# Row sums and squares in place of BN statistics, with a shifted edge: a fused gated-SSM and ternary FFN block

## The chip, the cores and the metric

The kernel runs on one core of a Trainium2 chip, in one launch. The metric is device time in microseconds, median of three executions. One more execution was recorded by the hardware profiler; every duration below comes from that one.

## The reference

The input is x, 8192 rows of 512 floats. Each layer is a norm, a block and a norm, with a residual around all three.

```python
x = x + _layernorm(attn(_layernorm(x)))
x = x + _layernorm(ffn(_layernorm(x)))
# attn: uv = x @ in_proj_w + in_proj_b; u, v = split(uv); v = silu(v)
#       v = 3-tap depthwise conv(v); h[t] = a*h[t-1] + ssm_b*v[t]; y = ssm_c*h + ssm_d*v
#       out = (u * silu(y)) @ out_proj_w + out_proj_b
#       h = out + residual; return layernorm(h) * ln_w + ln_b
# ffn:  h = gelu(x @ ternary(W1).T + b1);  return h @ ternary(W2).T + b2      (512 -> 2048 -> 512)
```

Between the two projections of one tile and its FFN stand three norms in a row: the norm inside `attn` (call it A, of out + residual), the norm around `attn` (B, whose input is A's output times ln_w plus ln_b), and the norm at the FFN's entrance (C, whose input is x1 = x + B). The second norm's input, in the words of the change, is the input of B.

## The kernel before

The 8192 rows are 16 tiles of 512 rows (`NT` = 16), each tile four blocks of 128 rows on the partitions (`NB` = 4, index j). All weights stay in SBUF. High precision comes from splitting a float into two float16 parts, `hi` (ScalarE) and `lo` (VectorE), so each projection is three matmuls where one would do.

The program is a software pipeline. In stage s, written `for s in LATER`, tile fa = s-2 is in its FFN, tile c = s-1 is in its SSM, out projection and norms A, B, C, tile n = s+1 is in its first norm and v projection, and tile e = s-3 gets the last touch of its FFN output and is stored. TensorE's order in a steady stage: nine f1 units of tile fa with five f2 units behind them (first half of the stage), the four u products of c, three more f2, the four o products of c, two v products of n, then f1 9 to 15 and the remaining f2, v 2 and 3, f2 12 to 15. `f1(t, j)` makes two hidden chunks for half a tile in bank `f1b`; ScalarE's `gelu` and `hi` and VectorE's `lo` make its float16 parts in `ring`; `f2(t, j)` multiplies them with W2 into the four banks `f2b`. f1 of unit i waits for gelu of i-2. u and o use two banks, `misc`, in turn: a product waits until the reader of the bank two products earlier is done (`gate` for u, `h_add` for o).

For tiles 2 to 12 (`seven(t)`), f2 is `f2_seven`: four plain matmuls over 512 columns for the `hi` part, and for the `lo` part seven half-size products in Strassen's manner, which need `combined` sums of W2 (made once, in `stage`) and four `presums` of two units of `h_lo`, made on VectorE (lines 970 to 977) just after `lo`. VectorE then takes the result apart with `drain`. Other tiles use plain products and `f_add`. Because tile fa's second half is drained in the next stage, `epilogue(e)` runs `f_add` or `drain`, `f_stats` and `aggr(4, ...)` early in it; GpSimd's `rstd_f` turns these into scales and ScalarE's `ffn_norm` waits for them.

The norms A, B, C of tile c on VectorE are `norms(c)`: `a1`, `a2` (A's output), `b_stats` and `aggr(2, ...)` (statistics of B's input), `x1`, `c_stats` and `aggr(3, ...)` (statistics of x1), `n3`. Between them GpSimd makes 1/sqrt of the variances (`rstd`, `rstd_b`), and afterwards the result is split (`t_hi`, `t_lo`) and transposed by DMA for the next f1.

The order on VectorE and ScalarE within a half stage is set by hand: each work item has a number (the `AT_` tables), and `run` sorts by it. The engines run their queues in order. An item that waits holds all behind it.

```python
def run(items):
    for _, work in sorted(items, key=lambda item: item[0]):
        work()
```

Stage 15 is special: tile 15 has no successor, so its SSM, u, o and `h_add` are done at the end of the same stage in which tile 14's norms run, and TensorE does all sixteen f2 units of tile 13 before them.

Of the kernel before, what the change touches and what calls it, by code (L numbers as in the profile page):

```python
# [63 lines left out]
AT_SILU_LAST, AT_GATE_LAST, AT_GATE_HI_LAST = 16.15, (15.0, 15.1), 16.5  # L64
AT_LO_LAST = (7.65, 8.95, 9.6, 10.6, 11.65, 12.2, 12.9)
# [36 lines left out]
def build(nc, x, w_in, w_out, w1t, w2t, params, rows, out):  # L102
# [42 lines left out]
    with ExitStack() as ctx:  # L145
# [389 lines left out]
        def _(pe):  # L535
# [50 lines left out]
            def o(c, j):  # L586

                out_ = take("o", c, j) if c > 0 else bank("o", 0, j)
# [58 lines left out]
            def f2_seven(t, j):  # L647
# [27 lines left out]
                product(f2b[0], right, s4, w2[:, p + PAIRS, right])
                product(f2b[1], left, a22, t4).then_inc(f2_mm, 1)

            def f2(t, j):
# [213 lines left out]
        def _(ve_):  # L892
# [37 lines left out]
            def f_add(e, j):  # L930
# [57 lines left out]
            def drain(t, h):  # L988
# [49 lines left out]
            def epilogue(e):  # L1038
# [1492 lines left out]
```

## Time and profile before

| | |
|---|---|
| median of 3 runs | 1414.5 us (1414.45 to 1415.38) |
| profiled execution | 1414.85 us, of which 1413.1 us span |
| TensorE busy | 1389.6 us, 98% |
| VectorE busy | 1208.9 us, 86% |
| ScalarE busy | 912.4 us, 65% |
| GpSimd busy | 371.8 us, 26% |
| TensorE clock granted | 0.999 of full speed |

A matmul's modelled end lies behind the start of the next, so short waits of TensorE do not show as idle time. They show as a start-to-start distance above the usual one. That usual distance is 0.216 us for 512 columns and 0.108 us for 256.

### The profile page before, as it was taken

How to read it: one execution, taken by the hardware profiler on the slowest of the kernel's cores; microseconds unless marked ns; L12 is line 12 of the kernel's file. 1: busy time of each engine (PE TensorE's matmuls, PEld its weight loads, DVE VectorE, ACT ScalarE, POOL GpSimd, SP SyncE). 2: the span in 40 equal slices, each digit the busy share in tenths (PEclk: the TensorE clock that was granted, in tenths of full speed). 3: DMA queues.
4: the chain of work that ended last, by engine and by line, in shares of the span. 5: the costliest groups of instructions: out<-in, count | busy, mean ns of one | idle time of the engine just before them, and what ended most of it. 6: DMA issues, size and time to landing. Idle time of an engine off the chain costs nothing.

```text
span 1413.1 us, 24900 instructions
## 1 busy us (share of the span) xinstructions
PE 1389.6 (98%) x8954; PEld 878.3 (62%) x8954; DVE 1208.9 (86%) x2360; ACT 912.4 (65%) x1504; POOL 371.8 (26%) x522
## 2 busy tenths in 40 slices
PE   7999999999999999999999999999999999999997
PEld 4444556657567675766757667675666757555664
DVE  7999988889889898888989889898898988898534
ACT  7999665756656565675656757566666656754543
POOL 5235242221412213132221412223132231313112
PEclk9999999999999999999999999999999999999999
DMA  8713530423304133232423305133141432202320
GB/s 237 256 45 90 137 54 19 109 42 91 60 12 109 31 90 61 45 75 31 107 44 91 51 11 120 31 90 60 26 96 31 97 53 61 31 1 63 58 30 31
DMA packets 164653, 98.12 MB, mean 69 GB/s; under 512 B 133681, under 2 KB 133681, under 8 KB 164401
## 3 DMA queue, kind: packets, MB, share of 16 engines
q1 hardware_dynamic: 155888, 80.79, 23.0%
q0 software_dynamic: 8640, 15.73, 8.2%
q8 instruction: 71, 1.16, 0.4%
q14 instruction: 54, 0.43, 0.1%
HBM read 31.49 MB, written 32.51 MB: 45 GB/s over the span
## 4 chain that ended last, share of the span: by engine, by line
PE 56%; DVE 19%; issue 11%; ACT 4%; POOL 3%; DVEq 0%; POOLq 0%; ACTq 0%
PE f1b L617 7%; PE f1b L618 7%; PE misc L580 5%; PE misc L582 5%; PE misc L581 5%; PE f2b L668 4%; DVE ring L926 4%; PE f2b L658 4%; PE misc L594 3%; PE f2b L641 3%; PE misc L596 3%; PE misc L595 3%; PE f2b L643 3%; DVE vl L1082 3%; DVE bn L908 2%
## 5 line engine op out<-in xcount | busy, mean ns | idle before, releaser
L618 PE MATMUL f1b<-x3T,w 128*128 128x256 f16 x1792 | 398.1, 273 | 0.0
L617 PE MATMUL f1b<-x3T,w 128*128 128x256 f16 x1792 | 398.1, 273 | 0.0
L1860 ACT ACTIVATE ring<-f1b,par 128x256 f32<-128x256 f32 x480 | 201.5, 471 | 208.3 <-PE f1b L618 208.0
L2297 POOL TENSOR_SCALAR ve<-mv 128x4 f32<-128x4 f32 (+2 forms) x89 | 46.9, 527 | 762.0 <-DVE mv L918 762.0
L926 DVE SCALAR_TENSOR_TENSOR ring<-ring,f_sc 128x512 f16<-128x512 f32 x256 | 188.0, 740 | 60.4 <-ACT ring L1874 60.4
L617 PEld LDWEIGHTS f1b<-x3T,w 128*128 128x128 fp8e5 x1792 | 175.4, 98 | 24.7 <-issue 0.4
L618 PEld LDWEIGHTS f1b<-x3T,w 128*128 128x128 fp8e5 x1792 | 175.3, 98 | 24.1
L1874 ACT ACTIVATE ring<-ring,f_sc 128x512 f16<-128x512 f32 x256 | 182.5, 720 | 0.0
L658 PE MATMUL f2b<-w,ring 128*128 128x512 fp8e5 x704 | 180.7, 379 | 0.0
L580 PE MATMUL misc<-x1T,win_hi 128*128 128x512 f16 x456 | 172.8, 379 | 1.8 <-DVE yb L1123 1.7
L582 PE MATMUL misc<-x1T,win_lo 128*128 128x512 f16 x456 | 172.8, 379 | 0.0
L581 PE MATMUL misc<-x1T,win_hi 128*128 128x512 f16 x456 | 172.8, 379 | 0.0
L1989 ACT ACTIVATE vb<-misc,par,inv_sig 128x512 f32<-128x512 f32 x54 | 41.9, 777 | 115.8 <-PE misc L582 115.7
L2354 POOL TENSOR_TENSOR hb<-hb,row 128x512 f32<-128x512 f32 x56 | 81.4, 1457 | 90.7 <-ACT hb L1921 90.7
L908 DVE BATCH_NORM_STATS2 bn<-hb 128x6 f32<-128x512 f32 x162 | 104.9, 680 | 0.2
L658 PEld LDWEIGHTS f2b<-w,ring 128*128 128x128 f16 x704 | 68.9, 98 | 50.2
L641 PE MATMUL f2b<-w,ring 128*128 128x512 fp8e5 x256 | 97.0, 379 | 0.9 <-DVE ring L926 0.8
L643 PE MATMUL f2b<-w,ring 128*128 128x512 fp8e5 x256 | 97.0, 379 | 0.0
L1082 DVE SCALAR_TENSOR_TENSOR vl<-vb,par,vl 128x512 f32<-128x512 f32 x128 | 92.4, 770 | 1.0 <-POOL vb L2403 0.8
L594 PE MATMUL misc<-wo_hi,g_hi 128*128 128x512 f16 x240 | 91.0, 379 | 0.4 <-DVE g_lo L1128 0.3
L595 PE MATMUL misc<-wo_lo,g_hi 128*128 128x512 f16 x240 | 91.0, 379 | 0.0
L596 PE MATMUL misc<-wo_hi,g_lo 128*128 128x512 f16 x240 | 91.0, 379 | 0.0
(263 smaller groups left out, 2695.1 us busy)
## 6 DMA issues: line engine op xcount, KB each, us to landing
out_dram<-xs SPq DMA_DIRECT2D x60, 256.0 KB, 2.9
xs<-x_dram SPq DMA_DIRECT2D x14, 1024.0 KB, 6.1
out_dram<-hb POOLq DMA_DIRECT2D x38, 256.0 KB, 5.2
out_dram<-stage POOLq DMA_DIRECT2D x22, 256.0 KB, 5.0
ring<-w1t_dram SPq DMA_DIRECT2D x3, 1024.0 KB, 12.3
stage<-w2t_dram SPq DMA_DIRECT2D x3, 1024.0 KB, 8.4
x1T<-tp SPq DMA_TRANSPOSE x68, 3.1
xs<-x_dram SPq DMA_DIRECT2D x4, 256.0 KB, 3.3
```

The lines of the kernel that those rows point to most:

```text
L580: pe.matmul(o[:, :], wh, x1T[:, s_, k, :], start=k == 0, stop=False)
L581: pe.matmul(o[:, :], wh, x1T[:, s_, KC + k, :], start=False, stop=False)
L582: mm = pe.matmul(o[:, :], wl, x1T[:, s_, k, :], start=False, stop=k == KC - 1)
L617: pe.matmul(o_, w, src[:, k, h * TH:(h + 1) * TH], start=k == 0, stop=False)
L618: mm = pe.matmul(o_, w, src[:, KC + k, h * TH:(h + 1) * TH], start=False, stop=k == KC - 1)
L641: pe.matmul(f2b[q][:, :], h_hi[:, i % H_SLOTS, qs], w2[:, chunk, :], start=chunk == 0, stop=False)
L643: mm = pe.matmul(f2b[q][:, :], h_lo[:, i % H_SLOTS, qs], w2[:, chunk, :], start=False, stop=chunk == FC - 1)
L658: pe.matmul(f2b[q][:, :], h_hi[:, r, n * TH + q * P:n * TH + (q + 1) * P], w2[:, chunk, :], start=p == 0 and n == 0, stop=False, skip_grou ...
L926: ve_.scalar_tensor_tensor(out=h_lo[:, i % H_SLOTS, :], in0=gg[:, i % G_SLOTS, :], scalar=f_sc[:, 0:1], in1=h_hi[:, i % H_SLOTS, :], op0=A ...
L1082: ve_.scalar_tensor_tensor(out=dst, in0=src, scalar=w, in1=dst, op0=ALU.mult, op1=ALU.add).then_inc(done, 1)
L1860: ins = act.activation(gg[:, i % G_SLOTS, ts], f1b[i % 2][:, ts], ACT.Gelu, bias=par[:, B1 + chunk:B1 + chunk + 1], scale=1.0 / ACT_SCALE)
L1874: act.activation(h_hi[:, i % H_SLOTS, :], gg[:, i % G_SLOTS, :], ACT.Copy, scale=f_sc[:, 0:1]).then_inc(hh_ok, 1)
```

## The change

Seven edits, named by letters.

(a) In `f2_seven` the wait for `sums_ok` moves back by three products: the three that use only `h_lo` come first, behind a wait for `hl_ok`. (b) `middle(t)` adds tile 1 to the tiles whose first output half is kept in `stage` (`hb_first`) and finished in the same stage. Tile 1's `f_add` and `f_stats` of blocks 0 and 1 move from stage 4 into stage 3, and those of blocks 2 and 3 stand before the scans. (c) For tiles 2 to 13 (`summed`) `a2` and `x1` write a row sum beside their result; `b_stats`, `c_stats` and their `aggr` are gone; ScalarE runs a Square with accumulation over each block, eight a tile; GpSimd makes the mean from the sum and the variance from the squares, with one more instruction for each norm. (d) In stage 15 three `lo` and two `t_lo` items and a gate change their places. (e) GpSimd's four `add_bias` of tile 15 go from behind tile 14's norms to two earlier places, behind waits for `a2` and `x1`. (f) The last out projection does three quarters of blocks 0 and 1, then their last quarters. (g) `h_add` of blocks 0 and 1 of tile 15 comes earlier among tile 13's `f_add`.

```diff
-AT_LO_LAST = (7.65, 8.95, 9.6, 10.6, 11.65, 12.2, 12.9)
+AT_LO_LAST = (7.65, 8.95, 9.6, 10.6, 11.6, 11.65, 12.2)
...
+AT_NORM_SUMS = ((7.7, 7.95, 8.2, 8.45), (8.7, 8.8, 8.9, 9.0), (11.7, 11.95, 12.2, 12.45), (14.7, 14.95, 15.2, 15.45))
+AT_B_SQUARE, AT_C_SQUARE = (9.05, 10.15, 11.15, 12.15), (13.15, 13.16, 14.15, 14.16)
...
+    def middle(t):
+
+        return 0 < t < NT - 3
+
+    def summed(c):
+
+        return 1 < c < NT - 2
...
-                pe.wait_ge(sums_ok, 4 * rank(i) + 4)
+                pe.wait_ge(hl_ok, i + 1)
...
                 product(f2b[0], left, a12, w2[:, p + PAIRS, left])
+                product(f2b[1], left, a22, t4)
+                pe.wait_ge(sums_ok, 4 * rank(i) + 4)
                 product(f2b[3], right, s1, t1, p == 0)
...
-                product(f2b[0], right, s4, w2[:, p + PAIRS, right])
-                product(f2b[1], left, a22, t4).then_inc(f2_mm, 1)
+                product(f2b[0], right, s4, w2[:, p + PAIRS, right]).then_inc(f2_mm, 1)
...
-                    for j in range(NB):
-                        o(NT - 1, j)
+                    o(NT - 1, 0, range(0, KC - 1))
+                    o(NT - 1, 1, range(0, KC - 1))
+                    o(NT - 1, 0, range(KC - 1, KC))
+                    o(NT - 1, 1, range(KC - 1, KC))
+                    o(NT - 1, 2)
+                    o(NT - 1, 3)
...
-                at = AT_F_STATS_NEXT if seven(e + 1) else AT_F_STATS
+                if middle(e):
+                    return (spread(AT_F_ADD, .2, [lambda j=j: f_add(e, j) for j in range(2, NB)])
+                            + spread(AT_F_STATS_SEVEN, .001, [lambda j=j: f_stats(e, j) for j in range(2, NB)])
+                            + spread(AT_F_STATS_SEVEN + .004, .001, [lambda j=j: aggr(4, e, j) for j in range(2, NB)]))
...
-                                             in1=lnb_row, op0=ALU.mult, op1=ALU.add).then_inc(a2_ok, 1)
+                                             in1=lnb_row, op0=ALU.mult, op1=ALU.add,
+                                             accum_out=sum_b[:, j:j + 1] if summed(c) else None).then_inc(a2_ok, 1)
...
+                if summed(c):
+                    at = AT_NORM_SUMS
+                    return [(at[k][j], lambda f=f, j=j: f(j)) for k, f in enumerate((a1, a2, x1, n3)) for j in range(NB)]
...
+                    gate_lo(NT - 1, 2)
                     gate(NT - 1, 3)
-                    gate_lo(NT - 1, 2)
+                    t_lo("t3", NT - 2, 1)
                     gate_lo(NT - 1, 3)
                     t_lo("t3", NT - 2, 2)
                     t_lo("t3", NT - 2, 3)
                     f_add(NT - 3, 0)
+                    h_add(NT - 1, 0)
+                    h_add(NT - 1, 1)
                     f_add(NT - 3, 1)
-                    h_add(NT - 1, 0)
...
+                src = hb_of(c)[:, j, :] if of_b else xs[:, c % X_SLOTS, j, :]
+                act.activation(spare[:, j % 2, :], src, ACT.Square, bias=sums[:, j:j + 1], scale=-float(D),
+                               accum_out=squares[:, j:j + 1], saturate=False).then_inc(done, 1)
...
+            def mean_of(sums, dst, made, c):
+
+                pool.wait_ge(made, NB * (c + 1))
+                link(pool.tensor_scalar(dst[:, :], sums[:, :], 1.0 / D, None, ALU.mult))
+
+            def rstd_sums(ln, squares, ready, c, dst, last):
+
+                pool.wait_ge(ready, NB * (c - 1))
+                link(pool.tensor_scalar(ve[:, ln, :], squares[:, :], 1.0 / D ** 3, EPS, ALU.mult, ALU.add))
+                ins = pool.tensor_tensor(dst, ve[:, ln, :], mhalf[:, :], ALU.pow)
...
+                if s == NT - 1:
+                    pool.wait_ge(a2_ok, NB * (c + 1))
+                    add_bias(NT - 1, 0)
+                    add_bias(NT - 1, 1)
                 if c is not None:
                     rstd_b(c)
+                if s == NT - 1:
+                    pool.wait_ge(x1_ok, NB * (c + 1))
+                    add_bias(NT - 1, 2)
+                    add_bias(NT - 1, 3)
```

**Place 1, edit (b).** VectorE's queue in the first half of stage 4, before, from the end of the second pair of taps (line 1082) over the first two scans (1091), `lo` and presums, to tile 1's FFN statistics (908, 918):

```order
L1082 SCALAR_TENSOR_TENSOR vl<-vb,par,vl 128x512 [waits tap0] x2
L1091 SCALAR_TENSOR_TENSOR vl<-a_par,carry,vl 128x512 [waits carry_ok,dv_ok,tap2]
L926 SCALAR_TENSOR_TENSOR ring<-ring,f_sc 128x512 [waits hh_ok]
L1091 SCALAR_TENSOR_TENSOR vl<-a_par,carry,vl 128x512 [waits carry_ok,dv_ok,tap2]
L926 SCALAR_TENSOR_TENSOR ring<-ring,f_sc 128x512 [waits hh_ok]
L974 TENSOR_TENSOR stage<-ring 128x2x128 [waits f2_mm,hl_ok]
L975 TENSOR_TENSOR stage<-ring 128x2x128
L977 TENSOR_TENSOR stage<-ring,stage 128x2x128 [waits sums_ok]
L970 TENSOR_TENSOR stage<-ring,stage 128x2x128 [waits sums_ok]
L908 BN_STATS bn<-hb 128x6 [waits mv_ok4,f_ok] x4
L918 BN_AGGR mv<-bn 128x2 [waits rs_ok4,bn_ok4] x4
```

The same place in the changed program, from the same taps on:

```order
L1113 SCALAR_TENSOR_TENSOR vl<-vb,par,vl 128x512 [waits tap0] x2
L935 BN_STATS bn<-hb 128x6 [waits mv_ok4,f_ok] x2
L945 BN_AGGR mv<-bn 128x2 [waits rs_ok4,bn_ok4] x2
L1122 SCALAR_TENSOR_TENSOR vl<-a_par,carry,vl 128x512 [waits carry_ok,dv_ok,tap2]
L953 SCALAR_TENSOR_TENSOR ring<-ring,f_sc 128x512 [waits hh_ok]
L1122 SCALAR_TENSOR_TENSOR vl<-a_par,carry,vl 128x512 [waits carry_ok,dv_ok,tap2]
L953 SCALAR_TENSOR_TENSOR ring<-ring,f_sc 128x512 [waits hh_ok]
L1003 TENSOR_TENSOR stage<-ring 128x2x128 [waits f2_mm,hl_ok]
L1004 TENSOR_TENSOR stage<-ring 128x2x128
L1006 TENSOR_TENSOR stage<-ring,stage 128x2x128 [waits sums_ok]
L999 TENSOR_TENSOR stage<-ring,stage 128x2x128 [waits sums_ok]
```

Four statistics behind the first two scans have become two in front of them; the other two now stand in stage 3.

**Place 2, edit (c).** ScalarE's queue in the second half of a steady stage of the changed program; `ring<-f1b` is a half of a gelu, `ring<-ring` is `hi`, `vl<-vb` is the centre tap of the next tile, and `xn,sq_b` and `xn,sq_c` are the squares:

```order
L1913 ACTIVATE ring<-ring,f_sc 128x512 [waits f2_mm,gelu_ok]
L1976 ACTIVATE xn,sq_b<-hb,sum_b 128x512 [waits bsq_ok,x1_lo,a2_ok]
L1899 ACTIVATE ring<-f1b,par 128x256 [waits hl_ok,f1_mm]
L1899 ACTIVATE ring<-f1b,par 128x256
L1913 ACTIVATE ring<-ring,f_sc 128x512 [waits f2_mm,gelu_ok]
L1976 ACTIVATE xn,sq_b<-hb,sum_b 128x512 [waits bsq_ok,x1_lo,a2_ok]
L1899 ACTIVATE ring<-f1b,par 128x256 [waits hl_ok,f1_mm]
L1899 ACTIVATE ring<-f1b,par 128x256
L1913 ACTIVATE ring<-ring,f_sc 128x512 [waits f2_mm,gelu_ok]
L1976 ACTIVATE xn,sq_c<-xs,sum_c 128x512 [waits bsq_ok,x1_lo,x1_ok] x2
L1938 ACTIVATE vl<-vb,par 128x512 [waits carry_ok,y_ok,v_ok] x2
L1899 ACTIVATE ring<-f1b,par 128x256 [waits hl_ok,f1_mm]
```

Without the rows that write `xn` this is the order before. The two first squares of x1 stand in front of two centre taps and a gelu, and they wait for VectorE's `x1` (the semaphore `x1_ok`).

**Place 3, edits (d) and (g).** VectorE's queue at the end of stage 15, before, from `lo` (926) of f2 unit 13 on; 1182 is `x1`, 1191 `n3`, 1123 `gate`, all as above:

```order
L926 SCALAR_TENSOR_TENSOR ring<-ring,f_sc 128x512 [waits hh_ok]
L1182 SCALAR_TENSOR_TENSOR xs<-hb,rsc,xs 128x512 [waits rs_ok2]
L1182 SCALAR_TENSOR_TENSOR xs<-hb,rsc,xs 128x512 x2
L926 SCALAR_TENSOR_TENSOR ring<-ring,f_sc 128x512 [waits hh_ok]
L1182 SCALAR_TENSOR_TENSOR xs<-hb,rsc,xs 128x512
L908 BN_STATS bn<-xs 128x6 [waits mv_ok3,x1_ok]
L926 SCALAR_TENSOR_TENSOR ring<-ring,f_sc 128x512 [waits hh_ok]
L908 BN_STATS bn<-xs 128x6 [waits mv_ok3,x1_ok] x3
L918 BN_AGGR mv<-bn 128x2 [waits rs_ok3,bn_ok3] x4
L1191 TENSOR_SCALAR hb<-xs,mv,rsc 128x512 [waits rs_ok3]
```

And in the changed program, from the same unit on:

```order
L953 SCALAR_TENSOR_TENSOR ring<-ring,f_sc 128x512 [waits hh_ok] x2
L1214 SCALAR_TENSOR_TENSOR xs<-hb,rsc,xs 128x512 [waits rs_ok2]
L1214 SCALAR_TENSOR_TENSOR xs<-hb,rsc,xs 128x512 x2
L953 SCALAR_TENSOR_TENSOR ring<-ring,f_sc 128x512 [waits hh_ok]
L1214 SCALAR_TENSOR_TENSOR xs<-hb,rsc,xs 128x512
L935 BN_STATS bn<-xs 128x6 [waits mv_ok3,x1_ok] x4
L945 BN_AGGR mv<-bn 128x2 [waits rs_ok3,bn_ok3] x4
L1225 TENSOR_SCALAR hb<-xs,mv,rsc 128x512 [waits rs_ok3]
L1154 SCALAR_TENSOR_TENSOR yb<-misc,bu_sig,yb 128x512 [waits u_mm,sy_ok]
L1225 TENSOR_SCALAR hb<-xs,mv,rsc 128x512
```

The `lo` of unit 14 has moved in front of the wait for `rs_ok2`, unit 15's has moved in front of the last `x1`, and a gate stands between the first two `n3`.

## Rows read from the trace of the kernel before

**Rows 1.** Busy time by window, core 0: a steady stage, stage 15, the rest.
```profile
682.08:767.42 85.34, 85.25 (x579) 56.24 (x576) 75.68 (x155) 54.88 (x92) 21.29 (x30) 1.00 0.30 62
...
1194.10:1293.24 99.14, 97.89 (x578) 55.91 (x576) 88.26 (x136) 57.11 (x96) 25.18 (x28) 1.00 0.22 47
1293.24:1413.10 119.86, 111.31 (x769) 75.05 (x767) 60.30 (x112) 56.20 (x111) 22.86 (x39) 0.99 0.20 36
```

**Rows 2.** Who waited for whom: total us, times, longest; weight loads of line 668.
```profile
PEld f2b L668 <- DVE stage L970: 8.6, 21, 0.6
```

**Rows 3.** Timeline, TensorE: start us, us, what [idle before <-releaser], stage 4.
```profile
282.57 0.38 PE L582 MATMUL misc<-x1T,win_lo 128*128 128x512 f16 x1
284.70 0.39 PE L580 MATMUL misc<-x1T,win_hi 128*128 128x512 f16 x1 [1.75 <-DVE yb L1123]
```

**Rows 4.** Timeline, VectorE and ScalarE, first half of stage 4.
```profile
268.70 2.47 DVE L908 BATCH_NORM_STATS2 bn<-hb 128x6 f32<-128x512 f32 x4
...
275.70 1.52 ACT L1885 ACTIVATE hb<-hb,nm,rs 128x512 f32<-128x512 f32 x2 [4.82 <-POOL nm L2329]
...
283.23 1.67 ACT L1926 ACTIVATE yb<-yb 128x512 f32<-128x512 f32 x3
...
283.89 1.41 DVE L1123 SCALAR_TENSOR_TENSOR yb<-misc,bu_sig,yb 128x512 f32<-128x512 f32 x2
```

**Rows 5.** Timeline, TensorE and VectorE, one f2 unit early in a steady stage.
```profile
782.90 1.03 PE L658 MATMUL f2b<-w,ring 128*128 128x512 fp8e5 x4
...
783.68 0.29 DVE L970 TENSOR_TENSOR stage<-ring,stage 128x256 f16<-128x256 f16 x1
...
784.03 0.39 PE L668 MATMUL f2b<-w,ring 128*128 128x256 fp8e5 x2
```

**Rows 6.** Timeline, TensorE, end of stage 15.
```profile
1266.73 0.38 PE L643 MATMUL f2b<-w,ring 128*128 128x512 fp8e5 x1
1267.95 0.39 PE L641 MATMUL f2b<-w,ring 128*128 128x512 fp8e5 x1 [0.84 <-DVE ring L926]
...
1283.93 0.39 PE L594 MATMUL misc<-wo_hi,g_hi 128*128 128x512 f16 x1 [0.31 <-DVE g_lo L1128]
```

**Rows 7.** Timeline, VectorE and GpSimd, end of stage 15.
```profile
1262.91 0.72 DVE L926 SCALAR_TENSOR_TENSOR ring<-ring,f_sc 128x512 f16<-128x512 f32 x1
1265.16 2.08 DVE L1182 SCALAR_TENSOR_TENSOR xs<-hb,rsc,xs 128x512 f32<-128x512 f32 x3 [1.52 <-POOL c L2321]
...
1273.36 2.90 DVE L1191 TENSOR_SCALAR hb<-xs,mv,rsc 128x512 f32<-128x512 f32 x2 [1.48 <-POOL rsc L2298]
...
1273.29 5.33 POOL L2354 TENSOR_TENSOR xs<-xs,row 128x512 f32<-128x512 f32 x4
```

**Rows 8.** Groups by line and shape: busy us, mean ns of one, idle before.
```profile
L908 DVE BATCH_NORM_STATS2 bn<-hb 128x6 f32<-128x512 f32 x162 | 104.9, 680 | 0.2
...
L1147 DVE SCALAR_TENSOR_TENSOR hb<-misc,o_inv,hb 128x512 f32<-128x512 f32 x56 | 41.7, 744 | 3.3 <-PE misc L596 2.2
...
L1182 DVE SCALAR_TENSOR_TENSOR xs<-hb,rsc,xs 128x512 f32<-128x512 f32 x60 | 41.3, 746 | 8.1 <-POOL c L2321 8.0
...
L918 DVE BATCH_NORM_AGGREGATE mv<-bn 128x2 f32<-128x6 f32 x320 | 40.9, 165 | 0.2
...
L1899 ACT ACTIVATE vl<-vb,par 128x512 f32<-128x512 f32 x64 | 48.9, 808 | 0.1
...
L1999 ACT ACTIVATION_READ_ACCUMULATOR w<-ring 128x1 f32 x4 | 0.8, 192 | 0.0
```

**Rows 9.** Timeline, ScalarE and VectorE, second half of a steady stage.
```profile
740.69 0.84 ACT L1860 ACTIVATE ring<-f1b,par 128x256 f32<-128x256 f32 x2 [0.56 <-PE f1b L618]
...
744.18 0.84 ACT L1860 ACTIVATE ring<-f1b,par 128x256 f32<-128x256 f32 x2 [0.30 <-PE f1b L618]
...
750.14 2.74 DVE L1182 SCALAR_TENSOR_TENSOR xs<-hb,rsc,xs 128x512 f32<-128x512 f32 x4 [0.48 <-POOL c L2321]
...
759.39 1.46 DVE L1191 TENSOR_SCALAR hb<-xs,mv,rsc 128x512 f32<-128x512 f32 x3 [1.47 <-POOL rsc L2298]
```

More of the change, by code:

```diff
@@ L372, in fo_pair @@
         def fo_pair(t, h):
-            return hb_first if seven(t) and h == 0 else hb[:, 2 * h:2 * h + 2, :]
+            return hb_first if middle(t) and h == 0 else hb[:, 2 * h:2 * h + 2, :]
         def fo(t, j):
@@ L584, in in_proj, with o @@
                     mm.then_inc(done, 1)
-            def o(c, j):
-                out_ = take("o", c, j) if c > 0 else bank("o", 0, j)
+            def o(c, j, ks=range(KC)):
+                out_ = take("o", c, j) if c > 0 and ks[0] == 0 else bank("o", c, j)
                 js = slice(j * P, (j + 1) * P)
@@ L591, in o @@
                     pe.wait_ge(wo_l, KC)
-                for k in range(KC):
+                for k in ks:
                     pe.wait_ge(glo_ok, KC * c + k + 1)
@@ L1761, in _ @@
                     gate_lo(c, 3)
-                parts = drain(fa, 0) if seven(fa) else []
+                parts = drain(fa, 0) if seven(fa) else [lambda j=j: f_add(fa, j) for j in range(2)] if middle(fa) else []
                 if n is not None:
@@ L1814, in _ @@
                 if c is not None:
-                    items += [(at, lambda j=j: t_lo("t3", c, j)) for j, at in enumerate(AT_T3_LO) if s < NT - 1 or j < 2]
+                    items += [(at, lambda j=j: t_lo("t3", c, j)) for j, at in enumerate(AT_T3_LO) if s < NT - 1 or j < 1]
                 if s == NT - 1:
@@ L1922, in residual, with square @@
                                scale=rs1[:, c % 4, j:j + 1]).then_inc(res_ok, 1)
+            def square(c, j, of_b):
+                sums, squares, made, done = (sum_b, sq_b, a2_ok, bsq_ok) if of_b else (sum_c, sq_c, x1_ok, csq_ok)
+                i = NB * (c - 2) + j
+                act.wait_ge(made, NB * c + j + 1)
+                act.wait_ge(x1_lo, NB * (c + 3))
+                if j >= 2:
+                    act.wait_ge(done, i - 1)
+                elif of_b and c > 2:
+                    act.wait_ge(csq_ok, i - j)
+                elif not of_b:
+                    act.wait_ge(bsq_ok, i - j + NB)
+                src = hb_of(c)[:, j, :] if of_b else xs[:, c % X_SLOTS, j, :]
+                act.activation(spare[:, j % 2, :], src, ACT.Square, bias=sums[:, j:j + 1], scale=-float(D),
+                               accum_out=squares[:, j:j + 1], saturate=False).then_inc(done, 1)
             def silu_y(c, b):
@@ L2235, in _ @@
                 if e is not None:
-                    items += [(at, lambda j=j: ffn_norm(e, j)) for j, at in enumerate(AT_F_NORM_SEVEN if seven(e) or seven(e + 1) else AT_F_NORM)]
+                    items += [(at, lambda j=j: ffn_norm(e, j)) for j, at in enumerate(AT_F_NORM_SEVEN if middle(e) else AT_F_NORM)]
                 if c is not None and s < NT:
@@ L2270, in _ @@
                     items += [(at, lambda b=b: centre_tap(s, b)) for b, at in enumerate(AT_CENTRE)]
+                if summed(c or 0):
+                    items += [(at, lambda j=j: square(c, j, True)) for j, at in enumerate(AT_B_SQUARE)]
+                    items += [(at, lambda j=j: square(c, j, False)) for j, at in enumerate(AT_C_SQUARE)]
                 if c is not None:
@@ L2488, in _ @@
                     rstd(1, c, rsc[:, 0, :], True)
+                if s == NT - 1:
+                    pool.wait_ge(a2_ok, NB * (c + 1))
+                    add_bias(NT - 1, 0)
+                    add_bias(NT - 1, 1)
                 if c is not None:
                     rstd_b(c)
+                if s == NT - 1:
+                    pool.wait_ge(x1_ok, NB * (c + 1))
+                    add_bias(NT - 1, 2)
+                    add_bias(NT - 1, 3)
+                if summed(c or 0):
+                    mean_of(sum_c, mean_c, x1_ok, c)
+                    rstd_sums(3, sq_c, csq_ok, c, rsc[:, 2, :], True)
+                elif c is not None:
                     rstd(3, c, rsc[:, 2, :], True)
-                if s == NT - 1:
-                    for j in range(NB):
-                        add_bias(NT - 1, j)
                 if n is not None:
```

56 lines of the change are left out of this document (39 added, 17 removed).

## The prediction

> **What bounds the kernel now.** I read the busy time by window first. In a steady stage TensorE is busy for 85.25 of 85.34 us, VectorE for 75.68, ScalarE for 54.88 [rows 1]. TensorE's stream sets the length of a stage; another engine matters only where TensorE waits for it. So the gain to be had is the sum of those waits, and I read the timeline of TensorE for start-to-start distances above 0.216 us (512 columns) or 0.108 us (256). Behind the start-up there are three kinds.
>
> First, one small stop in each of ten stages, at the weight loads of the f2 unit that opens a stage. The waits name it: line 668 behind VectorE's presum, 21 times, longest 0.6 us [rows 2]; most of the 8.6 us lie in weight loads that run ahead and cost nothing. On the timeline, the four matmuls from 782.90 are through at 782.90 + 4 x 0.216 = 783.76; the next starts at 784.03, since the last presum ended at 783.97 [rows 5]. That is 0.27 us, and I read 0.26 to 0.27 in the ten stages from 356.9 to 1124.9: 2.64 us together.
>
> Second, stage 4: 282.57 to 284.70 is 2.13 us where 0.22 is usual, so 1.91 lost, waiting for a gate [rows 3].
>
> Third, the end of stage 15: 1266.73 to 1267.95 is 1.22, so 1.01 lost behind a `lo`; before 1283.93 0.47 is lost behind a split gate [rows 6]; the same view has three smaller ones, 0.18, 0.18 and 0.23, nothing after that. Sum 2.07.
>
> All together 2.64 + 1.91 + 2.07 = 6.6 us. No edit takes work from TensorE, so 6.6 is about the most that the change can bring.
>
> **Edit (a), the order in `f2_seven`.** Same seven products. Those in front of the wait grow by three times 0.108 = 0.32 us. In the unit of [rows 5] the presums are then wanted at 783.76 + 0.32 = 784.08, and were ready at 783.97. The 0.27 us is covered with 0.11 to spare, if VectorE doesn't deliver later. Its queue ahead of that presum is not lengthened: the norms of the previous tile, shortened by (c), stand before it. Ten times 0.264: **-2.64 us**.
>
> **Edit (b), stage 4.** The chain is in [rows 4]: four statistics from 268.70 to 271.17, their four aggregations, GpSimd's scale; ScalarE's `ffn_norm` idles 4.82 us for it at 275.70 and holds `silu_y` behind it until 283.23; `gate` at 283.89 to 285.30; TensorE stands for 1.91. The change takes two `f_add` (0.74 each), two statistics (0.62) and two aggregations (0.08 start to start) from VectorE here, some 2.9 us, and puts the other statistics in front of the scans. Two scans and two `lo` (about 4 x 0.72 = 2.9 us) no longer stand before them. The scale is there some 4.5 to 5 us earlier, about the 4.82 that ScalarE idled, and the gate is wanted 1.9 us earlier. In the steady stages, whose statistics already stand in this place, the same wait is absent. Stage 3 pays for it: two `f_add`, two statistics and two aggregations more on VectorE, 2.9 us, while (c) takes more than that from the same half. **-1.91 us**.
>
> **Edit (c), sums and squares in twelve tiles.** VectorE loses eight statistics and eight aggregations. Four statistics in a row take 2.47 [rows 4], so 0.62 each; with 0.08 for an aggregation, 8 x 0.70 = 5.6 us a tile. It gains the output of eight sums. No row shows VectorE writing one. Bounds: 0, and 0.19 us, which ScalarE's own read of its accumulator takes as an instruction [rows 8]; I take 0.1, so 0.8 a tile, and VectorE is 4.8 us a stage lighter. ScalarE gains eight squares of 128x512. The nearest row is the activation of that size, 808 ns from start to modelled end [rows 8], about 0.63 to 0.71 from start to start, and about 0.1 for the accumulator: 8 x 0.75 = 6 us on 54.88 of 85.34 [rows 1]. GpSimd gets two small operations more, about 0.5 each. All three stay below TensorE, so there is no direct gain and no direct loss, but the order matters. Squares of B's input stand between a `hi` and the next gelu. In [rows 9] gelu waits for TensorE, by 0.56 at 740.69 and 0.30 at 744.18, so half of a square disappears in such idle time and the rest shifts gelu by about 0.1 to 0.4; `f1` of the unit after next wants it 0.7 us after it was done. Squares of x1 wait for VectorE's `x1` with two centre taps and a gelu behind them. `x1` at 750.14 waits 0.48 and `n3` at 759.39 waits 1.47 for GpSimd [rows 9]. Now the chain is: last `a2`, last square (about 747.1), GpSimd 2.2 us, `x1` at about 749.3; and `n3` at about 757.5. Both are earlier. The gelu behind the two squares comes 2.2 us later, but the f1 unit that takes its bank stands behind two v products and three f2 units and is not due before about 764. **0 us**; the cover is this slack of 0.7 us at the tightest gelu, and each 0.1 us beyond it costs 1.2 us in twelve tiles.
>
> The price of the sum bears on a rule. In [rows 8] the operation with two SBUF sources (line 1182, `x1`) takes 746 ns, that with a PSUM source (line 1147) 744: no sign that two SBUF sources are slower. The Trainium skill, "Vector Engine (DVE) Microarchitecture Reference", section 7, says that this kind of operation with two non-bf16 SBUF sources runs at half throughput, since both read ports are taken and none is left for the accumulator; the rows contradict it without a sum, and no row has one. What such a halving would do is rival B.
>
> **Edits (d), (e), (f), (g), stage 15.** The `lo` that TensorE waited for started at 1267.2 or so, behind three `x1` that had idled 1.52 for GpSimd; at 1262.91 VectorE had just done the previous `lo` and had that idle time to give [rows 7]. Now the next one stands in it: -1.01, and the one after it stands before the last `x1`: -0.18. The first two `n3` took 2.90 beside GpSimd's `add_bias` [rows 7], 1.45 each, against 1.46 / 3 = 0.49 in a steady stage [rows 9]; with `add_bias` elsewhere VectorE gains up to 1.9 us, `t_lo` and gates are earlier by as much, and the three smaller stops (0.18, 0.47, 0.23) close. That is -2.07. Against it: the split of the last o product puts the start of o(15, 2) behind o(15, 0) by only three matmuls of 0.216, 0.65 us, and it needs the bank that `h_add` of block 0 reads (0.74 us with its start). VectorE can begin only at the end of o(15, 0), so TensorE stands for about 0.35 including the semaphore. I put **-2.07 + 0.35 = -1.72**. What follows TensorE's end, some 8.5 us, stays.
>
> **Sum.** -2.64 - 1.91 + 0 - 1.72 = -6.27. The profiled execution took 1414.85 us (span 1413.1), so 1408.6; it lies 0.35 above the median of the runs, 1414.5, from which the sum gives 1408.2. I say 1408.3.
>
> **The rivals.** **B, the sum costs VectorE a second pass.** If `a2` goes from 0.66 to 1.2 us start to start, four of them delay the squares and, more, the `lo` and presums of f2 unit 8, ready at 744.0 before and wanted at 745.2 with edit (a); four times 0.54 with what queues behind gives about 745.4, 0.25 us a tile. Twelve tiles: +3.0, so 1411.3. The rows of [rows 8] speak against it, as far as they go. The Trainium skill's rule of the same section would give this case. Chance 0.12.
>
> **C, an edit frees only part of its stop.** In stage 4 `silu_y` could stay late because ScalarE's own `d_conv` and `hi` stand before it, in stage 15 the gates; the 1.52 and 1.48 us waits for GpSimd [rows 7] remain, and `add_bias` now stands before the `rstd(3)` that `n3` waits for. Half of 1.91 and half of 1.72 lost: +1.8, so 1410.1. Chance 0.12.
>
> **D, slower: the squares of x1 hold ScalarE.** They wait for `x1_ok` with gelu behind. Place: the second half of each of twelve tiles. The slack is the distance from the end of that gelu, about 758.8, to the next use at 764 or later, and 0.7 us at the earlier gelus. It decides once the chain a2, squares, GpSimd, x1 slips by more than that. If squares cost 1.5 us instead of 0.75, gelus of f1 10 to 13 are late by 0.8 to 1 us against 0.7, and four such waits a tile of 0.2 give 12 x 0.8 = 9.6: 1408.3 + 9.6 = 1418. For it: four squares of B's input stand in the densest part of ScalarE's queue. Against it: nothing in the rows puts an activation of this size above 0.81. Chance 0.05.
>
> **E, no gain in the steady stages.** Small shifts of gelu or `lo` open new stops of about 0.3 us as large as those closed: 2.6 + 1 back, so 1412. Chance 0.05.
>
> **How the numbers follow.** A measurement of this kernel tells 0.2%, 2.8 us, from no change: faster is below 1411.7, slower above 1417.3. My forecast, 0.66, with its own range 1407.4 to 1409.4: below, all 6.6 us plus 0.3 for gaps in the start-up; above, the 0.35 doubled and one of the small stops left. B 0.12 at 1411.3, C 0.12 at 1410.1, E 0.05 at 1412, D 0.05 at 1418. The range is 1407.3 to 1411.5: it takes in the forecast, C and most of B. Faster: the forecast, C, and most of B, 0.88; same: E and a part of B, 0.07; slower: D, 0.05.
>
> **What the profile of the changed kernel would show.** (a) Steady f2 units without a distance above 0.22 at the first products, or one of a few hundredths. (b) At 282 to 285 no gap, `ffn_norm`'s idle time below 1 us. (c) `a2` and `x1` still near 745 ns with a small extra each, VectorE's busy time in a steady stage about 71, ScalarE's about 61 to 62, a stage 85.07 us long instead of 85.34. (d) No idle time before line 641 at the place of 1267.95; (e) the first `n3` near 0.5 us each; (f) a new stop of 0.3 to 0.4 before o(15, 2). The prediction is wrong if a steady stage is longer than 85.15 us, above all if `a2` takes 1.2 us, if `gelu` waits for the squares of x1 into f1's time, or if stage 15 has a new wait behind `h_add` of more than half a microsecond.

## The result, and the profile after

The changed kernel takes 1409.13 us (median of 6 runs, 1407.68 to 1411.74), the kernel before on the same chip 1414.38 us (6 runs, 1413.37 to 1415.38). The ratio is 0.9963, 95% interval 0.9951 to 0.9975: 5.25 us, or 0.37%, faster. The profiled execution took 1408.3 us with a span of 1406.5, against 1414.85 and 1413.1. The six runs of the changed kernel spread over 4 us, so a median says less about the edits than the trace does.

In the trace I use one sum throughout: how far TensorE's start-to-start distances from 100 us on exceed 0.216 us (512 columns) or 0.108 us (256). It leaves out the start-up, which differs by 1 to 2 us between executions. Before, this sum is 12.56 us, of which 7.06 in stops above 0.1 us; after, it is 6.17, of which 0.72 in two stops. So the sum has fallen by 6.4 us, nearly all of it in stops, and two stops are left: 0.36 us at 109 us, which both kernels have, and 0.36 us in stage 15. One trace stands behind each kernel. Places that no edit touches move by up to 0.1 us between traces (the stop at 253.4 us, 0.12 here, is 0.11 with edit (a) alone and 0.22 with (d) to (g) alone), and one trace has a stop of 0.38 us that no other has. I therefore read a small difference at its place and not off the sum.

A steady stage is 85.10 us instead of 85.34 [rows 1] (busy time by window, columns as there: TensorE, its weight loads, VectorE, ScalarE, GpSimd, granted clock):

```profile
679.00:764.10 85.10, 85.10 (x579) 56.36 (x578) 70.82 (x146) 59.85 (x108) 21.93 (x32) 1.00 0.30 63
```

VectorE is 4.86 us a stage lighter, ScalarE 4.97 us heavier. In their stages tile 8's `x1` starts 1.5 us earlier than before and its `n3` 2.7 us earlier. TensorE's f2 unit that answers to [rows 5], with VectorE's last presum (timeline; start, duration):

```profile
779.47 1.03 PE L680 MATMUL f2b<-w,ring 128*128 128x512 fp8e5 x4
780.33 0.38 PE L690 MATMUL f2b<-w,ring 128*128 128x256 fp8e5 x2
780.55 0.27 PE L690 MATMUL f2b<-stage,ring 128*128 128x256 fp8e5 x1
780.66 0.49 PE L690 MATMUL f2b<-stage 128*128 128x256 fp8e5 x3
...
780.15 0.29 DVE L999 TENSOR_TENSOR stage<-ring,stage 128x256 f16<-128x256 f16 x1
```

The four plain matmuls (line 680) are through at 779.47 + 0.86 = 780.33, and the first product starts there. The sums end at 780.44, after that start and 0.22 us before 780.66, where the first product that reads them begins.

ScalarE in stage 4, against [rows 4], where `ffn_norm` idled 4.82 us:

```profile
270.61 1.51 ACT L1924 ACTIVATE stage<-stage,nm,rs 128x512 f32<-128x512 f32 x2
272.64 0.84 ACT L1899 ACTIVATE ring<-f1b,par 128x256 f32<-128x256 f32 x2 [0.53 <-PE f1b L640]
...
273.98 1.51 ACT L1924 ACTIVATE hb<-hb,nm,rs 128x512 f32<-128x512 f32 x2
...
279.39 2.19 ACT L1981 ACTIVATE yb<-yb 128x512 f32<-128x512 f32 x4
```

Both pairs of `ffn_norm` run without a wait, and the four `silu_y` run from 279.39 on, where before they began at 283.23. TensorE's stop of 1.91 us is gone.

VectorE at the end of stage 15, against [rows 7], and TensorE's one new stop:

```profile
1258.12 1.39 DVE L953 SCALAR_TENSOR_TENSOR ring<-ring,f_sc 128x512 f16<-128x512 f32 x2
1260.72 2.08 DVE L1214 SCALAR_TENSOR_TENSOR xs<-hb,rsc,xs 128x512 f32<-128x512 f32 x3 [1.21 <-POOL c L2399]
...
1268.25 0.55 DVE L1225 TENSOR_SCALAR hb<-xs,mv,rsc 128x512 f32<-128x512 f32 x1 [1.47 <-POOL rsc L2356]
1268.71 0.74 DVE L1154 SCALAR_TENSOR_TENSOR yb<-misc,bu_sig,yb 128x512 f32<-128x512 f32 x1
...
1280.93 0.38 PE L617 MATMUL misc<-wo_hi,g_lo 128*128 128x512 f16 x1
1281.51 0.39 PE L615 MATMUL misc<-wo_hi,g_hi 128*128 128x512 f16 x1 [0.20 <-DVE xs L1178]
```

Two `lo` now stand in front of the wait for GpSimd, `n3` takes 0.55 us, and the third o product waits for `h_add`: 1281.51 - 1280.93 - 0.22 = 0.36 us.

The operations of edit (c) (groups by line and shape: busy us, mean ns of one):

```profile
L1214 DVE SCALAR_TENSOR_TENSOR xs<-hb,rsc,xs 128x512 f32<-128x512 f32 x60 | 41.7, 747 | 12.7 <-POOL c L2396 11.4 <-POOL c L2399 1.2
L1203 DVE SCALAR_TENSOR_TENSOR hb<-hb,rsc,row 128x512 f32<-128x512 f32 x60 | 41.6, 746 | 0.0
...
L1976 ACT ACTIVATE xn<-hb,sum_b 128x512 f16<-128x512 f32 x48 | 35.0, 730 | 0.3 <-DVE hb L1203 0.3
...
L1976 ACT ACTIVATION_READ_ACCUMULATOR xn<-hb,sum_b 128x1 f32 x48 | 10.0, 208 | 0.0
...
L1203 DVE DVE_READ_ACCUMULATOR hb<-hb,rsc,row 128x1 f32 x48 | 4.0, 84 | 0.0
```

And how they follow each other (timeline, VectorE, one `a2` and the next, then ScalarE):

```profile
735.60 0.09 DVE L1203 DVE_READ_ACCUMULATOR hb<-hb,rsc,row 128x1 f32 x1
735.60 0.75 DVE L1203 SCALAR_TENSOR_TENSOR hb<-hb,rsc,row 128x512 f32<-128x512 f32 x1
736.27 0.09 DVE L1203 DVE_READ_ACCUMULATOR hb<-hb,rsc,row 128x1 f32 x1
...
736.58 0.72 ACT L1976 ACTIVATE xn<-hb,sum_b 128x512 f16<-128x512 f32 x1
737.19 0.20 ACT L1976 ACTIVATION_READ_ACCUMULATOR xn<-hb,sum_b 128x1 f32 x1
737.28 0.83 ACT L1899 ACTIVATE ring<-f1b,par 128x256 f32<-128x256 f32 x2
```

An `a2` with its row sum takes 0.67 us from start to start, and its accumulator is read in the same moment in which the next one starts. A square holds ScalarE for 737.28 - 736.58 = 0.70 us.

### The profile page after: what moved, and what is told of

The parts are those of the page before. It is cut to its first block, busy times and chain, and to the rows that moved or that the text cites. A ratio compares the mean times of both kernels' runs of the same rounds, so it can differ in the third digit from the quotient of the medians.

```text
span 1406.5 us, 24951 instructions
## 1 busy us (share of the span) xinstructions
PE 1386.9 (99%) x8954; PEld 879.9 (63%) x8954; DVE 1148.1 (82%) x2264; ACT 971.7 (69%) x1696; POOL 379.1 (27%) x546
## 4 chain that ended last, share of the span: by engine, by line
PE 92%; DVE 1%; issue 0%; ACT 0%; POOLq 0%; POOL 0%; DVEq 0%; ACTq 0%
PE f1b L639 15%; PE f1b L640 15%; PE f2b L680 11%; PE f2b L690 10%; PE misc L603 7%; PE misc L602 7%; PE misc L601 7%; PE f2b L665 4%; PE f2b L663 4%; PE misc L615 4%; PE misc L617 4%; PE misc L616 4%; PE f2b L722 1%; PE f2b L723 1%; PE f1b L645 0%; PE f1b L646 0%
## 5 line engine op out<-in xcount | busy, mean ns | idle before, releaser
L2355 POOL TENSOR_SCALAR ve<-mv 128x4 f32<-128x4 f32 (+2 forms) x65 | 35.5, 547 | 529.1 <-DVE mv L945 529.0
L1989 ACT ACTIVATE g_hi<-yb,g_sc 128x512 f16<-128x512 f32 x64 | 45.5, 716 | 71.2 <-DVE yb L1154 71.2
```

## The experiments

All times are medians beside the kernel before on the same chip (1414.36, 1414.40 and 1414.39 us in the three batches); "excess" is TensorE's sum from 100 us on. Edits are given against the kernel named.

| kernel | median us | ratio to before (95%) | excess us |
|---|---|---|---|
| before | 1414.4 | | 12.56 |
| changed | 1409.1 | 0.9963 (0.9951 to 0.9975) | 6.17 |
| (a) alone | 1411.6 | 0.9981 (0.9972 to 0.9990) | 9.83 |
| (b) alone | 1412.9 | 0.9988 (0.9979 to 0.9996) | 11.21 |
| (d) to (g) alone | 1412.6 | 0.9986 (0.9977 to 0.9995) | 10.76 |
| (c) alone | 1413.7 | 0.9994 (0.9985 to 1.0003) | 11.56 |
| changed without (c) | 1408.8 | 0.9965 (0.9953 to 0.9977) | 6.60 |
| changed without (f) | 1408.4 | 0.9964 (0.9951 to 0.9976) | 6.50 |
| changed without (e) | 1408.9 | 0.9963 (0.9949 to 0.9977) | 7.39 |
| changed, o in another bank | 1407.7 | 0.9959 (0.9946 to 0.9971) | 5.81 |
| changed, all squares twice | 1470.4 | 1.0395 (1.0381 to 1.0410) | 69.2 |
| changed, squares of B's input twice | 1421.9 | 1.0054 (1.0039 to 1.0069) | 20.06 |
| changed, squares of x1 twice | 1424.0 | 1.0068 (1.0053 to 1.0083) | 22.12 |

**(a) alone.** Against before:

```diff
-                pe.wait_ge(sums_ok, 4 * rank(i) + 4)
+                pe.wait_ge(hl_ok, i + 1)
...
+                product(f2b[1], left, a22, t4)
+                pe.wait_ge(sums_ok, 4 * rank(i) + 4)
                 product(f2b[3], right, s1, t1, p == 0)
```

> The kernel before with edit (a) alone. Theory: the three products cover the 0.27 us stop by themselves (margin 0.11 us), so the ten stops are gone and the span is 2.6 us shorter, time about 1411.8, VectorE as before. Rival: (a) needs the lighter VectorE of (c); the sums are then late by 0.1 to 0.2 us and a stop of that size is left ten times, gain only 1 to 2 us.

1411.58 us, excess 2.74 us down. None of the ten stops is left, the others stand as they were. The same unit as in [rows 5] (timeline, TensorE):

```profile
781.44 1.03 PE L658 MATMUL f2b<-w,ring 128*128 128x512 fp8e5 x4
782.31 0.38 PE L668 MATMUL f2b<-w,ring 128*128 128x256 fp8e5 x2
```

781.44 + 0.86 is 782.30: no gap. The edit needs no lighter VectorE.

**(b) alone.** Against before, with the branch for `middle` in `epilogue` and `f_add` as in the full diff:

```diff
+    def middle(t):
+
+        return 0 < t < NT - 3
...
-            return hb_first if seven(t) and h == 0 else hb[:, 2 * h:2 * h + 2, :]
+            return hb_first if middle(t) and h == 0 else hb[:, 2 * h:2 * h + 2, :]
```

> The kernel before with edit (b) alone. Theory: the 1.91 us stop in stage 4 is gone and stage 3 gets none, gain 1.9 us, time about 1412.5. Rival: the two more f_add, statistics and aggregations in stage 3 lie on a VectorE that (c) has not relieved, and a new stop of 0.3 to 1.9 us appears in stage 3 or 4; gain under 1.6 us.

1412.85 us. The 1.91 us stop is gone, but the excess falls by 1.35 only. At 253.3 us the stop before the first f1 of stage 4 has grown from 0.12 to 0.64, and one of 0.17 has come at 270.3, before products that read sums. The rival was right: VectorE in stage 3 isn't free without (c).

**(d) to (g) alone.** Against before, with the calls in stage 15 as in the full diff:

```diff
-AT_LO_LAST = (7.65, 8.95, 9.6, 10.6, 11.65, 12.2, 12.9)
+AT_LO_LAST = (7.65, 8.95, 9.6, 10.6, 11.6, 11.65, 12.2)
```

> The kernel before with edits (d), (e), (f), (g), all in stage 15. Theory: the five stops of 2.07 us go and one of 0.36 before the third o product comes, gain 1.7 us, time about 1412.7, independent of the rest. Rival: stage 15 is entered later or earlier relative to VectorE than with the others, and a stop of 0.2 to 0.5 us is left behind a lo.

1412.56 us, excess 1.80 down: five stops of 2.07 us gone, one of 0.36 new, so 1.71 in stops. The remaining 0.09 us is within what differs between traces.

**(c) alone.** The changed kernel with (a), (d) to (g) taken back as above, and (b) by:

```diff
     def middle(t):
-        return 0 < t < NT - 3
+        return 1 < t < NT - 3
```

> The kernel before with edit (c) alone. Theory: VectorE is about 4.5 us lighter and ScalarE 5 to 6 us heavier in each of twelve tiles, and TensorE's stops stay, those of line 668 at most 0.1 us smaller each because VectorE is a little earlier: span 0 to 1 us shorter, time 1413.5 to 1414.4, the 1.91 and the 2.07 us unchanged. Rival: the lighter VectorE already has the sums ready, the ten stops vanish with it and (a) would have been needless: 2.6 us shorter.

1413.68 us: not told from before by time. By the trace the excess is 1.00 down. Each of the ten stops is 0.17 to 0.18 instead of 0.26 to 0.27 (0.85 us in all), the one of 0.12 at 253.4 is gone, and those of stages 4 and 15 are unchanged.

**The changed kernel without (c).**

```diff
     def summed(c):
-        return 1 < c < NT - 2
+        return False
...
     def turn(ln, t):
-        return t - (max(0, t - 2) if t < NT - 2 else NT - 4) if ln in (2, 3) else t
+        return t
```

(`turn` gives the counts that the waits for statistics use.)

> The changed kernel with BN statistics in all tiles, so without edit (c). Theory: (c) bears nothing of the gain, TensorE has the same single stop of 0.36 us, span within 0.3 us of the changed kernel, time about 1408.4. Rival: (c) gave part of it, as the margin of the sums (0.11 us by the count) is used up, stops of 0.1 to 0.2 us in ten stages, 1 to 2 us slower than the changed kernel.

1408.8 us, the same by time. By the trace one stop has come back, 0.53 us at 253.4, before the first f1 of stage 4:

```profile
253.45 0.38 PE L665 MATMUL f2b<-w,ring 128*128 128x512 fp8e5 x1
254.20 0.27 PE L639 MATMUL f1b<-x3T,w 128*128 128x256 f16 x1 [0.37 <-issue]
```

It reads tile 2's transposed n3. The first `n3` of that tile starts at 246.75 here, at 244.32 with (c), and at 246.34 in the kernel before (timeline, VectorE, in this order; then TensorE before):

```profile
246.75 1.46 DVE L1225 TENSOR_SCALAR hb<-xs,mv,rsc 128x512 f32<-128x512 f32 x3 [1.24 <-POOL rsc L2356]
...
244.32 1.46 DVE L1225 TENSOR_SCALAR hb<-xs,mean_c,rsc 128x512 f32<-128x512 f32 x3 [1.21 <-POOL rsc L2385]
...
246.34 1.46 DVE L1191 TENSOR_SCALAR hb<-xs,mv,rsc 128x512 f32<-128x512 f32 x3 [1.24 <-POOL rsc L2298]
...
253.41 0.38 PE L643 MATMUL f2b<-w,ring 128*128 128x512 fp8e5 x1
253.75 0.27 PE L617 MATMUL f1b<-x3T,w 128*128 128x256 f16 x1
```

With (c) `n3` comes 2.4 us earlier, against a stop of 0.5. Against the kernel before, `n3` comes 0.41 us later here and the stop is 0.41 us longer. I read the wait from what f1 waits for in the code and from these times; the trace names no releaser.

**The changed kernel without (f).**

```diff
-                    o(NT - 1, 0, range(0, KC - 1))
-                    o(NT - 1, 1, range(0, KC - 1))
-                    o(NT - 1, 0, range(KC - 1, KC))
-                    o(NT - 1, 1, range(KC - 1, KC))
-                    o(NT - 1, 2)
-                    o(NT - 1, 3)
+                    for j in range(NB):
+                        o(NT - 1, j)
```

> The changed kernel with the four last o products whole and in order, so without edit (f). Theory: the 0.36 us stop before the third o product goes, and one behind the last split gate comes back, since g_lo of block 3 ends about 0.45 us before its place with the split and TensorE wants it three matmuls times three, 1.9 us, earlier: net 1 to 1.5 us slower. Rival: (e) and the moved gates already have that part ready, and the split only costs its 0.36 us: 0.3 us faster.

Neither: the 0.36 us stop is gone and one of 0.68 stands inside the first o product (at 1277.5), so the split is worth 0.32 us. I had the direction, not the size. The median, 1408.36, can't tell 0.3 us.

**The changed kernel without (e).**

```diff
-                if s == NT - 1:
-                    pool.wait_ge(a2_ok, NB * (c + 1))
-                    add_bias(NT - 1, 0)
-                    add_bias(NT - 1, 1)
...
-                if s == NT - 1:
-                    pool.wait_ge(x1_ok, NB * (c + 1))
-                    add_bias(NT - 1, 2)
-                    add_bias(NT - 1, 3)
...
+                if s == NT - 1:
+                    for j in range(NB):
+                        add_bias(NT - 1, j)
```

> The changed kernel with GpSimd's four add_bias of tile 15 behind tile 14's norms again, so without edit (e). Theory: the first two n3 take 1.45 us each again, gates and splits of stage 15 come up to 1.9 us later, and stops of 0.2 to 0.9 us in all come back before u and o products: 0.2 to 0.9 us slower. Rival: the order of gates and lo alone closes them, and the span is the same within 0.1 us apart from the start-up.

The first `n3` takes 1.49 us again, and stops of 0.11, 0.23 and 0.82 us stand in stage 15 in place of the 0.36: 0.8 us more, as expected. (The excess holds a further 0.38 us at 1068 us that no other trace has; what it waits for is open.)

```profile
1268.39 1.49 DVE L1225 TENSOR_SCALAR hb<-xs,mv,rsc 128x512 f32<-128x512 f32 x1 [1.47 <-POOL rsc L2356]
```

**Another bank for one o product.** The first of the last four goes to bank `f1b` 0, idle there; the third then waits for a gate only.

```diff
+                if (kind, t, i) == ("o", NT - 1, 0):
+                    pe.wait_ge(gelu_ok, FC * (NT - 2) - 1)
+                    return bank(kind, t, i)
+                if (kind, t, i) == ("o", NT - 1, 2):
+                    pe.wait_ge(reader["u"], 4 * (NT - 1) + i + 1)
+                    return bank(kind, t, i)
...
+                if (t, j) == (NT - 2, 0):
+                    pe.wait_ge(h_ok, NB * (NT - 1) + 1)
```

> The changed kernel with the first of the last four o products in the bank f1b 0, which is idle there, so that the third waits for a gate that was done long before and not for h_add. Theory: the last stop of 0.36 us goes, span 0.36 us shorter, time about 1408.0. Rival: the stop moves to the fourth o product or to the first f1 behind, and the time stays.

From 112 us to the end no stop above 0.1 us is left; the excess is 5.81, the least of all. 1407.66 us, 0.9959 of before: the best version run, though its interval overlaps that of the changed kernel.

**All squares twice.** This doubles the work of the step that the prediction's slower case rests on; the second result overwrites the first.

```diff
-                act.activation(spare[:, j % 2, :], src, ACT.Square, ...).then_inc(done, 1)
+                for k in range(SQUARES):
+                    ins = act.activation(spare[:, j % 2, :], src, ACT.Square, ...)
+                    if k < SQUARES - 1:
+                        extra[0] += 1
+                        ins.then_inc(again, 1)
+                        act.wait_ge(again, extra[0])
+                ins.then_inc(done, 1)
```

> The changed kernel with each Square done twice (the first result is overwritten), sixteen a tile. ScalarE gets about 6 us more in each of twelve stages. Theory by the margins of f1 behind gelu in the changed kernel (0.68, 2.02 and 3.36 us at the units 12, 13 and 14): the gelus are late by 0.75, 1.5 and 2.2 us, so 0.1 us is lost at unit 12 and what the longer chain to x1 and n3 brings is hidden: 1 to 2 us slower in all. Rival, the slower case of the prediction: the squares of x1 hold gelu and hi of units 13 and 14 past their use, 0.8 us or more a tile, 10 us slower or more.

1470.4 us, 61 us slower than the changed kernel. Both expectations fall. The gelus give way where the margins said, at f1 unit 12, by one stop of 0.22 us a tile (2.4 us in all). The large loss is elsewhere, eleven times in this form (timeline, TensorE; then VectorE one tile later, 90 us on):

```profile
611.09 1.04 PE L682 MATMUL f2b<-w,ring 128*128 128x512 fp8e5 x4 [0.21 <-ACT ring L1915]
...
612.21 0.27 PE L692 MATMUL f2b<-stage,ring 128*128 128x256 fp8e5 x1
615.36 0.82 PE L692 MATMUL f2b<-stage 128*128 128x256 fp8e5 x3 [2.88 <-DVE stage L1001]
...
616.19 1.91 PE L682 MATMUL f2b<-w,ring 128*128 128x512 fp8e5 x4
...
696.92 0.29 DVE L1001 TENSOR_TENSOR stage<-ring,stage 128x256 f16<-128x256 f16 x1
699.99 1.46 DVE L1227 TENSOR_SCALAR hb<-xs,mean_c,rsc 128x512 f32<-128x512 f32 x3 [2.77 <-POOL rsc L2395]
701.36 0.75 DVE L955 SCALAR_TENSOR_TENSOR ring<-ring,f_sc 128x512 f16<-128x512 f32 x1
...
705.19 0.29 DVE L1001 TENSOR_TENSOR stage<-ring,stage 128x256 f16<-128x256 f16 x1
```

VectorE stands 2.77 us at `n3`, which waits for GpSimd's scale, which waits for ScalarE's last square. Behind `n3` in its queue are the `lo` and the presums of f2 units 14 and 15, and TensorE stands for them 3.04 us. The chain from `a2` to `n3` has become 6.4 us longer: 3.15 from `a2` to `x1`, 3.26 from `x1` to `n3`.

Then the clock. After that stop four matmuls of 512 columns take from 616.19 to 617.89, 0.43 us each and not 0.22: TensorE runs at 1.2 GHz (busy time by window; the last three columns are granted clock, DMA share and GB/s):

```profile
612.30:615.30 3.00, 0.18 (x2) 0.00 (x0) 2.93 (x8) 2.97 (x5) 0.00 (x0) 0.93 0.49 94
615.40:618.90 3.50, 3.50 (x16) 1.96 (x17) 3.01 (x5) 2.37 (x3) 0.32 (x2) 0.58 0.80 154
619.00:622.00 3.00, 3.00 (x30) 2.69 (x28) 2.93 (x7) 0.84 (x2) 0.00 (x0) 1.00 1.18 292
```

The mean granted clock of the window behind the stop is 0.58; it is 0.50 from 614.9, shortly before the stop ends, to 618.3. The sum over the excess: 11 x 3.04 = 33.5 for the stop, 4.1 for one of 0.37 just ahead of it, 14.5 for half-clock stretches in eight of the eleven tiles, 2.2 for a stop of 0.73 in the three others, 2.4 at unit 12, 4.7 in stage 3, the rest small.

**Either half of the squares twice.** In the kernel above, `SQUARES` for B's input and for x1 apart; (1, 2) in the second run:

```diff
-SQUARES = 2
+SQUARES = (2, 1)
```

> The changed kernel with only the four squares of B's input done twice. In the run with all eight doubled, x1 and n3 together came 6.4 us later than before behind a2, TensorE stood 3.4 us a tile for presums whose lo stands behind n3, and ran at half clock for some 3 us after it. Theory: one chain with a slack of about 3.0 us decides; this half lengthens it by 3.15, so 0.1 to 0.4 us a tile, no clock drop, 2 to 5 us slower than the changed kernel, about 1412. Rival, linear: each half gives half of the 61 us, about 1440; and if the gelus between these squares were what counts, nearly all of it, 1460.

> The changed kernel with only the four squares of x1 done twice. Theory of one chain with 3.0 us of slack: this half lengthens it by 3.26, so 0.2 to 0.4 us a tile, no clock drop, 3 to 5 us slower than the changed kernel, about 1412 to 1413. Rival, linear: about 1440; and if the squares of x1 that hold ScalarE were the cause by themselves, nearly all of it, 1460.

1421.88 and 1423.97 us: 13 and 15 us slower than the changed kernel, together 28, where both at once cost 61. The linear rivals fall, and so does the size that I gave, 2 to 5 us. The granted clock does not fall in either trace before TensorE's last matmul. The stop at units 14 and 15 is 0.18 and 0.53 us, so the slack of the chain is 3.15 - 0.18 = 3.0 and 3.26 - 0.53 = 2.7 us; with B's squares twice there is the stop of 0.22 at unit 12 too. What I had missed is a second stop, 0.73 us a tile in both (and 0.14 ahead of it with x1's squares), in the first half of the next stage. It is the unit of edit (a) (squares of x1 twice, timeline):

```profile
703.59 0.27 PE L692 MATMUL f2b<-stage,ring 128*128 128x256 fp8e5 x1
704.42 0.50 PE L692 MATMUL f2b<-stage 128*128 128x256 fp8e5 x3 [0.56 <-DVE stage L1001]
```

`n3` delays VectorE's t_lo, the taps of the next tile and the drain behind them. Its first `lo` of the stage, which in the changed kernel idles 1.01 us for ScalarE, then has nothing left to idle, and everything behind it is about 1 us late. The slack at that unit is the 0.22 us read above.

## Why the prediction was right, and where it was not

**The total.** Forecast 1408.3, range 1407.3 to 1411.5; measured 1409.13, and 1408.3 in the profiled execution, for which the sum gave 1408.6. 6.4 us of excess went, of 6.27 predicted. That the profiled execution hits 1408.3 to the tenth is luck, since the start-up alone differs by 1 to 2 us between executions. Term by term the stops give 2.59 (ten stops, put at 2.64) + 1.91 + 2.07 - 0.36 = 6.21, and 0.12 at 253.4 that the sum didn't hold. Of the difference to the median, 0.8 us, nothing shows in the traces' stops; in these six runs it goes with the granted clock: 1407.7 to 1408.5 at 0.999, 1409.8 and 1410.0 at 0.998, 1411.7 at 0.997. In the eleven runs of (a) alone it does not: the slowest, 1413.6, has 0.999.

**Edit (a): -2.64, right.** Shown alone: the ten stops, 2.59 by the trace, are gone, and the excess is 2.74 down. The sums were to have 0.11 us to spare; in the unit shown they have 0.14 with (a) alone (ready at 782.49, read from 782.63) and 0.22 with (c).

**Edit (b): -1.91, right with (c), wrong alone.** "(c) takes more than that from the same half" was the condition that I named, and it is needed: alone the edit gives -1.35.

**Edit (c): 0 us on TensorE, nearly.** The relief of VectorE was put at 4.8 us a stage and is 4.86. ScalarE's addition was put at 6 and is 4.97, a square at 0.75 and is 0.70. The sum's price was put at 0.1 us, between 0 and 0.19, and is about 0.01 from start to start: the read (84 ns) lies beside the next operation. With that price the same count gives 5.5 us for VectorE, so the hit at 4.8 is partly luck. Taken by groups, statistics and aggregations free 5.5 us of VectorE's time and the other operations count about 0.6 more; on ScalarE the squares add 5.8 and the others count about 0.7 less. My reading, not shown: the modelled end of an operation counts as busy only where no other operation starts in it, and (c) shifts which operations stand before idle time. But (c) isn't worth nothing. I saw that `n3` comes earlier and gave it no value, though TensorE had a stop of 0.12 us at 253.4 that I left out of the count; with (b) it would be 0.53. In the changed kernel (c) is worth 0.4 us of 6.4.

**Rival B, the second pass, does not exist here.** `a2` and `x1` take 748 ns in the 48 cases each that write a row sum and 739 and 741 ns in the 12 each of the same trace that don't; before, 745 and 746 [rows 8]. From start to start it is 0.67 us with the sum and 0.66 before. (The group lines above mix the 48 and the 12.) The Trainium skill, "Vector Engine (DVE) Microarchitecture Reference", section 7, states half throughput for this operation with two non-bf16 SBUF sources, for want of a port for the accumulator. This trace contradicts it for these operands, float32 from SBUF with and without the sum; the measurement decides.

**Stage 15: -1.72, right term by term.** -2.07 and +0.36 against -2.07 and +0.35; alone the same stops, -1.71. Within it (e) carries 0.8 us and the split 0.3.

**Rival C didn't happen:** no stop was left half open. **Rival D was placed and priced wrongly**, which the result alone would never have shown. "Gelus of f1 10 to 13 are late" was its step, with 0.7 us of slack and 9.6 us for a square of twice the length. Doubling the squares costs 61 us. The gelus do give way at 0.7 us, for 2.4 us in all. The step that fails is that the price stands there: the chain a2, squares, GpSimd, x1, squares, GpSimd, n3 has `lo` and presums queued behind its last wait, with 2.7 to 3.0 us of slack for TensorE, and its delay also runs on through VectorE's queue to a unit with 0.22 us. I had asked who waits behind the squares on ScalarE, and not who waits behind `n3` on VectorE.

## What to carry to other kernels

On a kernel whose main engine never pauses, sum the start-to-start excess of that engine's instructions: it shows stops of 0.1 us that busy time hides, it is free of the start-up, and read stop by stop it tells edits of 0.3 us apart where the median of runs that spread over 4 us cannot. Off the sum alone it would not: one trace had 0.38 us more at a place that no edit touched. An edit that frees an engine off the critical path is worth little by itself (1.0 us for 4.9 us a stage) but can carry another edit's cost, so test it alone and left out. And before work is put into a chain between engines, follow every queue behind each wait of that chain to the next use on the main engine: half the added work cost 13 and 15 us, all of it 61.

## What I had not expected of the hardware

VectorE's `scalar_tensor_tensor` on float32 gives a row sum for about 0.01 us: 748 ns with it against 745 before, 0.67 us from start to start against 0.66, the accumulator's read of 84 ns beside the next instruction. On ScalarE the read takes 188 to 208 ns, of which 0.09 us are on the path.

A stop of about 3 us cost TensorE more than itself: in eight of eleven cases a stretch at 1.2 GHz followed, together 112 matmuls that lost 14.5 us. The granted clock fell between 1.05 us before the stop's end and 1.2 us behind it. No shorter stop had such a stretch: not the one of 1.91 us in stage 4 of the kernel before, nor those of up to 1.25 us in stage 3 with all squares doubled, nor those of 0.73 us a tile. Why three of the eleven stops had none is open.
